# Attention probabilities in two tiles instead of one, with the key order turned when PSUM is read, and a new order of all work

## The reference

```
xn = layernorm(x)
# branch 1: causal attention, 16 heads of 64
q, k, v = xn @ W_qkv;  q, k = rotary(q), rotary(k)
scores  = q @ k.T / 8, masked to -1e9 where key > query
out     = softmax(scores) @ v @ W_out
# branch 2: 16 heads of 8 without a mask, layernorm, then a mixture of 8 experts (top 2), layernorm
x = x + out + ffn(xn)
```

## Time and profile before

| | us |
|---|---|
| median of 3 runs | 1407.32 |
| range of the runs | 1400.66 to 1414.51 |
| the profiled execution | 1420.66 |
| span in its trace, first to last instruction | 1418.8 |

### The profile page before, as it was taken

How to read it: one execution, slowest core, us unless ns; L and a number is a source line. 1 busy time by engine, 2 the same in 40 slices (tenths; PEclk the granted TensorE clock), 3 DMA queues, 4 the chain that set the end, 5 groups by cost and what they waited for, 6 DMA issues and landing times.

```text
span 1418.8 us, 23791 instructions
## 1 busy us (share of the span) xinstructions
PE 1110.0 (78%) x8474; PEld 662.9 (47%) x8474; DVE 1034.0 (73%) x2404; ACT 742.4 (52%) x1665; POOL 857.6 (60%) x728
## 2 busy tenths in 40 slices
PE   4778789687886878887798777877889678897866
PEld 2334446344452444544464444544546335463534
DVE  6966679767786767965788657777768766787646
ACT  3656455564544645555455644547545464555731
POOL 3658766657665485576564756656676555744940
PEclk8799979899798978988889886998969888698978
DMA  5163632455224442434524363244542245425342
GB/s 158 41 135 86 147 88 60 108 127 119 64 73 110 116 121 60 96 87 116 123 64 108 83 147 77 68 104 112 124 108 71 72 96 119 112 64 123 81 93 66
DMA packets 77793, 139.27 MB, mean 98 GB/s; under 512 B 11494, under 2 KB 23016, under 8 KB 77676
## 3 DMA queue, kind: packets, MB, share of 16 engines
q1 hardware_dynamic: 74204, 134.80, 39.8%
q10 hardware_dynamic: 3472, 2.95, 0.7%
HBM read 5.60 MB, written 2.10 MB: 5 GB/s over the span
## 4 chain that ended last, share of the span: by engine, by line
PE 36%; DVE 20%; DMA 17%; SPq 12%; POOL 7%; issue 4%; ACT 3%; ACTq 1%; POOLq 0%; DVEq 0%
DMA pt<-pn 12%; PE work L1708 10%; SPq L1140 10%; DVE fnmax L1458 7%; PE work L1758 4%; PE work L1694 4%; DVE pn L1588 4%; DMA swapped<-raw 4%; PE work L1616 3%; PE work L1724 3%; PE work L1618 3%; PE work L1617 3%; PE work L1733 3%; DVE work L1540 2%; DVE branch L1543 2%
## 5 line engine op out<-in xcount | busy, mean ns | idle before, releaser
L1196 POOL TENSOR_TENSOR raw<-raw,cos_t 128x512 f32<-128x512 f32 x128 | 163.5, 1277 | 406.4 <-DMA swapped<-raw 390.5
L1293 ACT ACTIVATE fpt<-work 128x1024 f32<-128x1024 f32 x256 | 251.9, 1026 | 202.0 <-PE work L1748 192.7
L1458 DVE TENSOR_REDUCE fnmax<-work 128x2 f32<-128x1024 f32 x256 | 302.4, 1215 | 59.1 <-PE work L1733 58.0
L1338 ACT ACTIVATE pn<-work,nmax 128x512 f32<-128x512 f32 (+3 forms) x512 | 266.0, 537 | 140.5 <-DVE nmax L1580 139.8
L1708 PE MATMUL work<-pt,v 128*32 128x384 f32 (+2 forms) x2560 | 211.9, 493 | 118.0 <-DMA pt<-pn 113.1
L1580 DVE CUSTOM_DVE_ANT_0 work<-work,causal 128x512 f32<-128x512 f32 (+3 forms) x512 | 236.6, 515 | 81.2 <-PE work L1694 80.8
L1708 PEld LDWEIGHTS work<-pt,v 128*32 128x32 f32 x2560 | 100.2, 136 | 228.4 <-issue 154.7
L1588 DVE STREAM_TRANSPOSE pn<-pn 128x1024 f32<-128x1024 f32 (+1 forms) x192 | 198.6, 1048 | 3.3 <-ACT pn L1338 3.2
L1211 POOL TENSOR_TENSOR qk_l<-raw,qk_h 128x512 fp32r<-128x512 f32 x128 | 180.0, 1413 | 3.4
L1200 POOL TENSOR_TENSOR raw<-raw,swapped 128x512 f32<-128x512 f32 x128 | 164.3, 1284 | 10.0
L1197 POOL TENSOR_TENSOR swapped<-swapped,sin_t 128x512 f32<-128x512 f32 x128 | 164.6, 1286 | 0.0
(11 more groups left out here) (153 smaller groups left out, 1893.0 us busy)
## 6 DMA issues: line engine op xcount, KB each, us to landing
pt<-pn SPq DMA_DIRECT2D x256, 320.0 KB, 5.7
swapped<-raw SPq DMA_DIRECT2D x256, 128.0 KB, 2.3
fqs<-fqn SPq DMA_DIRECT2D x96, 128.0 KB, 2.7
x_in<-in_L_attn_x_dram SPq DMA_DIRECT2D x8, 256.0 KB, 4.7
out_dram<-x_in SPq DMA_DIRECT2D x7, 256.0 KB, 2.3
fpt<-in_L_attn_W_qkv_dram ACTq DMA_DIRECT2D x3, 512.0 KB, 6.2
pn<-in_L_ffn_We_dram ACTq DMA_DIRECT2D x1, 512.0 KB, 9.7
wout<-in_L_attn_W_out_dram ACTq DMA_DIRECT2D x1, 512.0 KB, 12.5
```

Of the source, the lines that this page charges most:

```text
L1196: nc.gpsimd.tensor_tensor(raw[:, n % 3], raw[:, n % 3], cos_t[:], ALU.mult)
L1293: nc.scalar.activation(fpt[:, ((b * G + g) * T + i) % FP, 2 * r:2 * r + 2].rearrange("p h n -> p (h n)"), bank_of(("fst", b, g, i), 2 * r, 2),
L1338: ins = nc.scalar.activation(pn[:, c % 2, :, h, tiles].rearrange("p c i r -> p i c r"), bank_of(("sc", b, c, unit), h)[:, at:at + n].rearr ...
L1458: nc.vector.tensor_reduce(fnmax[:, j, 2 * r:2 * r + 2, 0:1], bank_of(("fsm", b, g, j), 2 * r, 2).rearrange("p (f n) -> p f n", f=2), AX.X, ...
```

## The change

1. pn and pt become two tiles each. The first holds units 0 and 1 (8 query-key tiles: runs of 2048 bytes), the second unit 2 (2 tiles: runs of 512 bytes). "shuf" moves the first and waits for the transpose of unit 1; the new step "shu2" moves the second and waits for the transpose of unit 2. Both wait for "pv" of pair c-1. There are eight DMAs per pair instead of four, and the bytes are the same. The bands go in the order 0, 2, 1, 3.
2. GpSimd writes k in plain order. "exp" reads PSUM with a step of four numbers inside a tile instead, and writes pn as before.
3. "pv" can't take tiles of pn's two parts in one matmul: 28 float32 matmuls (56 instructions) for a pair instead of 20 (40), over the same 1280 columns. 256-column matmuls go from 4 to 12, 128-column ones from 8 to 16, and the eight 384-column ones go.
4. At the start, two small tables are loaded elsewhere and one copy of the mask on VectorE goes.
5. PLACE and the banks are new throughout.

```diff
-PT_N = T * (T + 1) // 2
+PT_N = [2 * T, T // 2]
+PT_OF = {3: (0, 0), 2: (0, T), 0: (0, 2 * T - 1), 1: (1, 0)}
...
-                elif kind == "shuf":
-                    c = x_[2]
-                    wait(sp, after("tr", b, c, 2))
+                elif kind in ("shuf", "shu2"):
+                    c, part = x_[2], int(kind == "shu2")
+                    wait(sp, after("tr", b, c, 1 + part))
                     wait(sp, after("pv", *ring(1, b, c, NC)))
-                    for a in range(QUADS):
-                        sp.dma_start(pt[:, a].rearrange("p h n r -> p (h n r)"),
-                                     pn[a * STRIP:(a + 1) * STRIP, c % 2].rearrange("p c h n r -> p c (h n r)")).then_inc(shuf_done[c % 2], 16)
+                    for a in (0, 2, 1, 3):
+                        sp.dma_start(pt[part][:, a].rearrange("p h n r -> p (h n r)"),
+                                     pn[part][a * STRIP:(a + 1) * STRIP, c % 2].rearrange("p c h n r -> p c (h n r)"))                            .then_inc((shuf_done, shu2_done)[part][c % 2], 16)
...
-                    nc.gpsimd.tensor_copy(turned(qk_h[:, c % 2, k], k), plain(raw[:, n % 3], k)).then_inc(done["hi"], 1)
+                    nc.gpsimd.tensor_copy(qk_h[:, c % 2, k], raw[:, n % 3]).then_inc(done["hi"], 1)
...
-                                                   bank_of(("sc", b, c, unit), h)[:, at:at + n].rearrange("p (i c r) -> p i c r", r=STRIP, c=QUADS),
+                                                   bank_of(("sc", b, c, unit), h)[:, at:at + n].rearrange("p (i r c) -> p i c r", r=STRIP, c=QUADS),
...
                     wait(pe, landed("shuf", b, c))
+                    wait(pe, landed("shu2", b, c))
...
-                    for i, js in ((0, (3, 2, 1)), (0, (0,)), (1, (3, 2, 1)), (2, (3, 2)), (3, (3,))):
+                    for i, js in ((0, (3, 2)), (0, (0,)), (0, (1,)), (1, (3, 2)), (1, (1,)), (2, (3, 2)), (3, (3,))):
...
     "tr": [
...
-        [463, 470, 477, 482, 496, 497, 505, 506, 515, 532, 534, 535, 545, 551, 552, 555, 556, 559, 574, 577, 578, 589, 594,
+        [462, 471, 480, 486, 499, 501, 504, 516, 519, 531, 532, 536, 545, 546, 550, 556, 557, 559, 574, 576, 579, 589, 591,
```

More of the change, by code:

```diff
@@ L58 @@
         [0],
-        [78],
-        [197],
+        [77],
+        [200],
         [326],
-        [456],
-        [585],
+        [461],
+        [586],
         [716],
-        [842],
+        [846],
     ],
@@ L85 @@
         [86],
-        [213],
+        [215],
         [342],
-        [472],
+        [473],
         [601],
         [729],
-        [858],
+        [859],
     ],
     "fv": [
[L94 to L101, removed]
+        [7],
+        [119],
+        [244],
+        [381],
+        [510],
+        [634],
+        [760],
+        [898],
     ],
     "fsm": [
[8 rows of a table removed]
[8 rows of a table added]
     ],
     "fmT": [
-        [14, 30, 58, 83],
@@ L115 @@
[L115 to L121, removed]
+        [13, 29, 60, 83],
+        [131, 153, 189, 214],
+        [259, 281, 316, 341],
+        [388, 411, 446, 472],
+        [515, 540, 577, 600],
+        [645, 668, 705, 730],
+        [774, 798, 834, 858],
+        [903, 928, 963, 986],
     ],
     "fst": [
[8 rows of a table removed]
[8 rows of a table added]
     ],
     "fpv": [
[8 rows of a table removed]
[8 rows of a table added]
@@ L205 @@
         [617, 679],
-        [747, 808],
-        [876, 937],
-        [1002, 1033],
+        [746, 807],
+        [875, 937],
+        [1006, 1033],
     ],
@@ L251 @@
         [164, 168, 169, 171],
[L252 to L258, removed]
+        [293, 297, 299, 301],
+        [422, 426, 427, 430],
+        [551, 556, 557, 559],
+        [680, 684, 685, 687],
+        [809, 813, 814, 816],
+        [938, 941, 944, 946],
+        [1027, 1028, 1030, 1032],
     ],
@@ L267 @@
         [3],
[L268 to L273, removed]
+        [78],
+        [199],
+        [319],
+        [452],
+        [574],
+        [700],
         [826],
@@ L291 @@
         [85],
-        [210],
-        [336],
-        [462],
+        [209],
+        [335],
+        [461],
         [587],
@@ L415 @@
     "gexp": [
-        [156],
-        [283],
+        [157],
+        [284],
         [409],
@@ L420 @@
         [661],
-        [787],
-        [913],
-        [1011],
+        [788],
+        [914],
+        [1009],
     ],
@@ L427 @@
         [12],
-        [98],
-        [264],
-        [391],
-        [542],
-        [704],
+        [101],
+        [259],
+        [386],
+        [538],
+        [702],
         [847],
@@ L435 @@
     "turn": [
-        [8],
+        [7],
     ],
     "str": [
-        [4],
-    ],
-    "xn": [
-        [2],
-        [40],
-        [216],
-        [364],
-        [509],
-        [650],
-        [801],
-        [945],
-    ],
-    "strl": [
-        [5],
-    ],
+        [2],
+    ],
+    "xn": [
+        [3],
+        [69],
+        [215],
+        [365],
+        [508],
+        [652],
+        [804],
+        [944],
+    ],
+    "strl": [
+        [4],
+    ],
     "wl": [
-        [1, 7, 21],
+        [1, 5, 21],
     ],
@@ L459 @@
         [91],
-        [227],
+        [232],
         [375],
-        [526],
-        [669],
-        [812],
-        [959],
+        [525],
+        [671],
+        [817],
+        [965],
     ],
     "sml": [
-        [3],
+        [11],
     ],
     "qkb": [
-        [9],
+        [8],
     ],
     "bia": [
-        [11],
+        [10],
     ],
     "wel": [
-        [27],
+        [29],
     ],
     "fqkl": [
-        [10],
+        [9],
         [99],
         [244],
-        [390],
-        [536],
-        [681],
-        [828],
-        [974],
+        [389],
+        [535],
+        [682],
+        [827],
+        [971],
     ],
     "fmax": [
[1 row of a table removed]
[1 row of a table added]
          82, 92, 93],
[3 rows of a table removed]
[3 rows of a table added]
          346, 366, 367, 368, 369, 372, 373, 383, 384],
[10 rows of a table removed]
[10 rows of a table added]
     ],
@@ L589 @@
     "yadd": [
-        [116, 188],
-        [263, 332],
-        [408, 479],
-        [554, 624],
-        [702, 772],
-        [845, 916],
-        [991, 1062],
+        [116, 186],
+        [262, 334],
+        [409, 479],
+        [554, 626],
+        [701, 771],
+        [845, 917],
+        [993, 1062],
         [1134, 1176],
@@ L599 @@
     "cl": [
-        [157],
+        [156],
         [302],
-        [449],
+        [448],
         [595],
-        [740],
-        [887],
-        [1031],
-        [1144],
+        [741],
+        [886],
+        [1030],
+        [1145],
     ],
     "ln1": [
-        [163],
-        [308],
-        [455],
+        [162],
+        [307],
+        [454],
         [601],
-        [746],
-        [893],
-        [1040],
+        [747],
+        [892],
+        [1037],
         [1149],
@@ L635 @@
         [906],
-        [1052],
-        [1161],
+        [1050],
+        [1160],
     ],
     "gsub": [
-        [182],
-        [327],
+        [181],
+        [326],
         [473],
@@ L645 @@
         [911],
-        [1057],
-        [1165],
+        [1055],
+        [1164],
     ],
     "pick": [
-        [183],
+        [182],
         [328],
         [474],
-        [620],
-        [766],
-        [912],
-        [1058],
+        [621],
+        [765],
+        [913],
+        [1057],
         [1167],
@@ L679 @@
     "nm2": [
-        [229],
-        [360],
-        [520],
+        [213],
+        [363],
+        [511],
         [666],
-        [813],
-        [948],
-        [1094],
+        [801],
+        [991],
+        [1092],
         [1178],
@@ L696 @@
         [0],
-        [10],
-        [35],
-        [122],
-        [159],
-        [201],
-        [270],
-        [336],
+        [9],
+        [42],
+        [126],
+        [180],
+        [209],
+        [280],
+        [316],
     ],
     "rope": [
[8 rows of a table removed]
[8 rows of a table added]
     ],
     "hi": [
[8 rows of a table removed]
[8 rows of a table added]
     ],
     "lo": [
[8 rows of a table removed]
[8 rows of a table added]
     ],
     "rs1": [
-        [60],
-        [111],
+        [59],
+        [113],
         [168],
-        [221],
-        [273],
-        [329],
-        [385],
-        [425],
+        [223],
+        [275],
+        [330],
+        [381],
+        [426],
     ],
@@ L746 @@
         [62],
-        [113],
-        [172],
-        [222],
-        [275],
-        [331],
-        [386],
+        [114],
+        [169],
+        [225],
+        [277],
+        [333],
+        [385],
         [428],
@@ L756 @@
         [68],
-        [119],
-        [180],
+        [120],
+        [179],
         [234],
-        [288],
-        [342],
-        [394],
+        [284],
+        [337],
+        [395],
     ],
     "rs2": [
-        [76],
-        [127],
-        [186],
-        [240],
-        [294],
-        [346],
-        [402],
+        [74],
```

(79 more changed lines are left out.)

269 lines of the change are left out of this document (131 added, 138 removed), and 427 rows, old and new, of tables (PLACE, PSUM).

## The result

The changed kernel takes 1480.89 us (median of 4 runs, 1473.22 to 1486.06), the kernel before 1406.02 beside it: a ratio of 1.052, interval 1.045 to 1.059. The forecast was 1368 us, the range ended at 1425.

The account below looks back on a forecast made before the run. Bound by waits between engines working in order, 22% of the chain (312 us) at shuffles. Terms -80 + 13 - 5 + 6 = -66 us, 60% counted as -40 us, 2.8% off the median 1407.3: 1368 us, range 1325 to 1425.

Parts of the forecast that it names:

- part 5: SyncE's queue and the rest: 256 more issues, 0.1 us a pair, +6 us (-10 to +40); the order itself not costed.
- the head start g: Shuffle held up by the transpose: first tile leaves g earlier, saving 1.5 + g, at most 5.5 us; 3.5 taken.
- Part 1: Split shuffle and band order 0, 2, 1, 3: saves 80 us on the chain in 28 shuffles, bounds 20 and 130.
- 60% of it: Share of the summed -66 us expected to come home, since something else is late next: -40 us.
- rival 2: Split does nothing, "shuf" held by "pv" of the pair before; only band order saves, 14 us, about 1393; chance 0.20.
- part 2: "pv" on TensorE: 16 more instructions a pair, 19 us more busy time, +13 us on the chain (0 to 97).
- The signs: Signs expected: "pt<-pn" and issues from 22% to some 15% of the chain, TensorE's wait from 113 to under 70 us.
- rival 1: Shuffle was the true bound, TensorE also keeps its clock: 80 to 110 us less, about 1310; chance 0.13.
- Part 3: GpSimd writes k in plain order: 50 us less of GpSimd, worth -5 us (0 to -20).
- Part 4: "exp" on ScalarE reading PSUM with a step: taken as 0, upper bound +226 us of ScalarE.
- Rival 3: ScalarE pays for the step in PSUM, lengthening "exp" before each shuffle: 1480 us; chance 0.10.
- Rival 4: SyncE's queue: small DMAs wait while the first tile drains, swaps 1 to 1.5 us later; about 1440; chance 0.07.

Follow-up runs that it names:

- experiment 1: The changed kernel's code with the order tables and PSUM banks of the kernel before: 1330.71 us, ratio 0.937 to the kernel before.
- experiment 2: The code of the kernel before with the changed kernel's tables, its one shuffle at the later of the two places: 1588.29 us, ratio 1.122.
- experiment 3: The changed kernel with "shuf" and "shu2" swapped in SyncE's queue in the 16 pairs where "shu2" stood first: 1434.12 us, ratio 1.011.
- experiment 13: The kernel of experiment 1 with "div" 1.5 places earlier on VectorE: 1357.28 us, ratio 0.953 to the kernel before.
- experiment 7: The changed kernel with SyncE's queue in the old order, "shu2" right behind "shuf", engines in the new order: 1419.03 us, ratio 1.002.
- experiment 6: The kernel before with only "pv" changed, to 28 matmuls (56 instructions) instead of 20: 1419.88 us, ratio 1.002.
- experiment 5: The kernel before with GpSimd writing k plainly and "exp" reading PSUM with a step of four: 1413.71 us, ratio 0.998.
- 9: The new code with the old engine orders and SyncE's queue sorted by readiness in a trace: 1318.92 us, ratio 0.935 to the kernel before.
- 10: The changed kernel, engines in the new order, with SyncE's queue sorted by readiness in a trace: 1375.47 us, ratio 0.972 to the kernel before.

## Why the prediction was wrong

The step that failed is one sentence of part 5: "The order itself I can't cost; it is about the same one." It got the value 0 in the sum and no part in the range. It was worth 12% (experiments 1 and 2), the largest term by far and larger than everything that was worked out. I had even counted that "shu2" stands ahead of "shuf" in 16 pairs and that "div" comes two steps earlier, and priced neither. The first: in such a pair the large tile waits for the small one's transpose, so the head start g is not smaller but gone: the tile that could go waits 9.4 us on average in these 16 pairs. It measured 4 points (experiment 3). The second means that VectorE stands at "div" for a "pv" that isn't there yet, with the maxima of the next pair behind it. It measured 1.6 points for 1.2 steps (experiment 13). VectorE's wait for "pv" of 232.1 us in the changed kernel is mostly not due to it, since with the old queue and the same place of "div" it is 88.9 us (experiment 7).

**Part 1, split and band order.** The mechanism was right and the size too small: with the old tables all of the code gives 6.3%, where I had -66 us and 60% of it, 2.8%. The band order alone gives 3.3%, some 47 us; rival 2, where it is alone, had 42 us on the chain and after deductions 14. The 60% is the larger part of the shortfall, the +13 us of part 2 the rest: without both the sum is -79 us, and 6.3% are 89. (A slip in the working changes nothing: 1.2 + 0.26/115 + 0.79/250 gives 6.6 us, not 6.7.)

The saving was less for each shuffle and came at more of them: from all that it waits for to its last byte a shuffle takes 8.0 us in experiment 1 against 9.9 before, 2.0 us less as a mean of 64 pairs, where the sum had 80 us in 28 of them, 2.9 each. The signs came in part: TensorE's wait for pt fell to 55.8 us (under 70 forecast), but the move and its issues kept 21% of the chain (15% forecast). "About twice as fast" for reading both halves was too much as a price: a DMA of the old size lands in 4.9 us instead of 5.7.

What I took for an upper case, in rival 1, happens: the clock. A "pv" of 56 instructions takes 4.03 us or 2.41 us in the same kernel, that of experiment 1 (chain in order of time, then the same stretches with their busy times, granted clock, DMA share and GB/s):

```profile
608.50 4.03 PE work L1710 x56
...
632.46 2.41 PE work L1710 x56
...
608.50:612.53 4.03, 4.03 (x60) 2.74 (x60) 0.00 (x0) 0.28 (x1) 2.77 (x3) 0.58 0.56 143
632.46:634.87 2.41, 2.41 (x60) 1.86 (x60) 0.35 (x1) 0.00 (x0) 0.00 (x0) 1.00 0.00 0
```

and all of TensorE's 9498 instructions hold it busy for these times, in experiment 1 and in the changed kernel (page of each):

```profile
PE 1070.5 (81%) x9498; PEld 685.4 (52%) x9498; DVE 1031.0 (78%) x2403; ACT 741.1 (56%) x1665; POOL 812.4 (61%) x728
```

against 1126.5 us above. The granted clock is 0.887 of full speed on average in the one and 0.842 in the other. The instructions are the same; the 56 us come from running more of them at the lower level (1.2 instead of 2.4 GHz). Of the 64 "pv", 47 run wholly at the full clock in experiment 1 and 2 wholly at the half one; in the changed kernel it is 19 and 22, in the kernel before 27 and 10. Ahead of the 22 TensorE had stood still for 4.6 us on average, ahead of the 19 for 0.5 (worked out from the trace). So a shorter wait pays for itself and again in the clock, and a longer one costs again: from experiment 6 to experiment 1, with the same 9498 instructions in the same order, TensorE's busy time falls from 1104.2 to 1070.5 us, 34 us. This counts work of TensorE, not all of which is on the chain. No discount of 40% was due; something nearer to none.

**Part 2, the matmuls.** +13 us were taken from busy times by shape; experiment 6 gives nothing (1.002, its upper end 8 us). The groups by shape overlap each other in time, 268 us in sum where "pv" as a whole is busy for 211.9, so their differences aren't prices.

**Part 3, GpSimd.** -5 us; nothing measured (0.998, experiment 5).

**Part 4, "exp".** The value 0 was right: 535 ns against 537. Rival 3 falls: that its 1480 us are the measured time is chance, for its cause measured nothing (experiment 5). The Trainium skill's line on non-contiguous patterns in PSUM (PSUM — Partial Sum Buffer, "Specifications (TRN2)") doesn't carry over to ScalarE's reads here.

**Part 5, the queue.** Rival 4 named the right place, SyncE's queue and the swaps, with a chance of 0.07 and a wrong mechanism; its sign, a longer wait of GpSimd for the swaps, came (500.5 us) and would have misled. Issuing isn't the trouble: experiment 1 has the same 256 more DMAs and GpSimd waits 345.9 us for its swaps, less than the 390.5 of before. The part of the trouble that is shown in this queue is a step in a strict queue that waits for something late while ready ones stand behind it.

**What is left open.** How the 12% of the tables divides depends on the queue that one compares with. With the queue in its old order the engines' orders and banks cost 7% (experiment 1 to 7), and the new queue 5% on top (1.002 to 1.052). Against queues sorted by readiness it is 4% for the engines and banks (9 to 10) and 8% for the new queue (0.972 to 1.052). So a part lies in how queue and engines fit. Of the engines' share "div" explains some; which other steps hold it, and whether the banks have a part, stays open.

## What to carry to other kernels

When a change comes with new tables of order, the order is a term of the sum: read for each strict queue which step stands ahead of which, and ask of each pair that changed places what the first waits for and how long the second has then been ready. A split that lets a part go early gives no head start in a queue that has the late part ahead of it. Try the two halves of such a change apart, the code in the old order and the order with the old code; here one was worth 6% less time and the other 12% more, and the changed kernel alone showed neither.

## What the runs showed of the hardware that was not expected

In a shuffle of four DMAs that each read 32 partitions, a DMA lands after 4.9 us (median) against 5.7, 14% sooner, when consecutive ones read from different halves of the 128 partitions, with nothing else changed. ScalarE reads PSUM with a step of 16 bytes as fast as in a row (535 and 537 ns). GpSimd's cast of 512 numbers takes 0.61 us when it writes them in a row and 1.13 when it writes them 128 bytes apart. And "pv" in 56 instructions takes 2.35 to 2.38 us at a granted clock of 1.00 (47 times in experiment 1), where the same columns in 40 took 2.34 to 2.37 (27 times in the kernel before), so the number of instructions hardly counts. At a granted clock of 0.50 it is 4.49 to 4.50 us in either form.
